# Three stages around a bounded attention layer: one block for the middle stage, weights loaded in the front, another order of steps in the attention periods

## The reference, cut to what matters

```python
h = _L0_tok_ref(x, L0_tok_W)
h = jnp.concatenate([h, _L0_txt_ref(...)], axis=1)
h = h + _L0_attn_ref(_layernorm(h), ...)
h = h + _L0_ffn_ref(_layernorm(h), ...)
```

## Time and profile before

| | |
|---|---|
| time of three runs | 2068.76, 2068.5, 2061.65 us, median 2068.5 |
| the profiled execution | 2066.16 us, span from first to last instruction 2064.1 us |
| busy share of the span | PE 70%, DVE 44%, ACT 35%, POOL 27% |
| mean granted TensorE clock | 0.788 of full |
| instructions | 33321 |

### The profile page before, as it was taken

One profiled execution on the slowest core, in us unless ns is written; L12 is line 12 of the kernel. 1 busy time (PEld: TensorE's weight loads), 2 busy tenths in 40 slices (PEclk: granted clock), 3 DMA queues, 4 the chain that ended last, 5 costly groups with the idle time before them and its releaser, 6 DMA issues.

```text
span 2064.1 us, 33321 instructions
## 1 busy us (share of the span) xinstructions
PE 1443.6 (70%) x11676; PEld 703.7 (34%) x11676; DVE 904.6 (44%) x1638; ACT 721.5 (35%) x837; POOL 552.5 (27%) x738
## 2 busy tenths in 40 slices
PE   6774203994100736998879888888898888889963
PEld 6442103994100512333333333333333333333321
DVE  1125534004753452636436545544544544643343
ACT  0100000112100003575365365365455446447640
POOL 3777202000211001223133133232322322232331
PEclk9886656996555557899799799789889889879985
DMA  6792062872031045071051052062052052044000
GB/s 106 146 192 62 9 165 95 300 264 50 0 70 9 6 80 68 17 125 23 36 87 41 22 90 43 9 110 44 10 109 44 10 99 54 10 83 63 1 13 6
DMA packets 147574, 142.94 MB, mean 69 GB/s; under 512 B 85261, under 2 KB 112693, under 8 KB 147395
## 3 DMA queue, kind: packets, MB, share of 16 engines
q1 hardware_dynamic: 133090, 136.03, 30.4%
q0 software_dynamic: 4352, 2.43, 0.7%
q10 hardware_dynamic: 9984, 2.51, 0.6%
HBM read 110.73 MB, written 25.44 MB: 66 GB/s over the span
## 4 chain that ended last, share of the span: by engine, by line
PE 39%; DVE 17%; issue 6%; SPq 2%; ACT 2%; POOL 2%; DMA 1%; DVEq 0%; POOLq 0%; ACTq 0%
PE b_pso L1656 13%; PE b_pss L1632 10%; PE b_psm L1678 4%; PE b_psm L1702 3%; PE b_psm L1690 3%; ACT b_pb L1736 2%; PE b_pss L1630 2%; DVE b_rq L1901 1%; PE b_psm L1600 1%; POOL b_pb L1776 1%; PE b_psm L1685 1%; PE b_psm L1682 1%; PE b_psm L1707 1%; DVE b_h L1900 1%; DVE b_tmp L1959 1%
## 5 line engine op out<-in xcount | busy, mean ns | idle before, releaser
L1736 ACT ACTIVATE b_pb<-b_pss 128x1024 f32<-128x1024 f32 (+2 forms) x736 | 663.5, 937 | 719.3 <-PE b_pss L1632 563.2
L1776 POOL TENSOR_SCALAR_AFFINE_SELECT b_pb<-b_pb 128x256 f32<-128x256 f32 (+1 forms) x544 | 240.4, 461 | 880.1 <-ACT b_pb L1736 873.8
L1656 PE MATMUL b_pso<-b_pb,b_vop 128*32 128x77 f32 (+4 forms) x5376 | 416.8, 420 | 71.1 <-POOL b_pb L1776 54.9
L1632 PE MATMUL b_pss<-b_qop,b_kop 97*128 97x512 bf16 (+3 forms) x1536 | 371.6, 365 | 41.1 <-issue 18.5
L1632 PEld LDWEIGHTS b_pss<-b_qop,b_kop 97*128 97x128 bf16 x1536 | 125.7, 106 | 283.5 <-ACT b_pb L1736 122.1
L1656 PEld LDWEIGHTS b_pso<-b_pb,b_vop 128*32 128x32 f32 x5376 | 118.6, 117 | 273.6 <-issue 200.5
L580 PE MATMUL psc<-tz,ub 128*32 128x128 f32 x2304 | 128.4, 278 | 75.5 <-DVE ub L613 75.5
L580 PEld LDWEIGHTS psc<-tz,ub 128*32 128x32 f32 x2304 | 127.5, 110 | 76.4 <-issue 75.7
L1982 DVE TENSOR_TENSOR b_ofm<-b_pso,b_mk 128x512 f32<-128x512 f32 (+1 forms) x96 | 51.8, 540 | 223.3 <-PE b_pso L1656 220.0
L1870 DVE COPY b_ot<-b_psm 128x336 f32<-128x336 f32 (+1 forms) x96 | 40.2, 419 | 181.1 <-PE b_psm L1678 180.9
L1757 POOL TENSOR_TENSOR b_stat<-b_stat,b_mh 128x18 f32<-128x18 f32 x32 | 107.3, 3369 | 38.8 <-DVE b_stat L2039 27.3
(11 more groups left out here) (318 smaller groups left out, 1548.7 us busy)
## 6 DMA issues: line engine op xcount, KB each, us to landing
tz<-taps SPq DMA_DIRECT2D x64, 576.0 KB, 4.7
b_qop<-qk_parts_b SPq DMA_DIRECT2D x192, 144.0 KB
stream<-in_x SPq DMA_DIRECT2D x16, 1024.0 KB, 12.7
qk_parts_b<-b_qs SPq DMA_DIRECT2D x16, 864.0 KB, 5.0
b_kop<-qk_parts_b SPq DMA_DIRECT2D x192, 36.0 KB
b_mk<-b_mskf SPq DMA_DIRECT2D x128, 36.0 KB, 3.8
qk_parts_b<-b_ks SPq DMA_DIRECT2D x8, 432.0 KB, 3.9
h<-h ACTq DMA_DIRECT2D x9, 256.0 KB, 4.1
```

The source lines that it names most:

```text
L1632: mm = pe.matmul(pss[:, u % 2, b, col:col + w], lhs, qop[:, n, e, q0:q0 + w], start=True, stop=True, skip_group_check=True)
L1656: mm = pe.matmul(pso[VW * ee:VW * (ee + 1), (3 * n + x) % 2, q0 - QT * x:q0 - QT * x + w], vop[0:r, j, n, :], pb[0:r, slot_, b, cc:cc + w] ...
L1736: nc.scalar.activation(pb[:, s % PB, 0:nb, 0:w], pss[:, s % 2, 0:nb, 0:w], ACT.Exp, scale=float(HD) ** 0.5).then_inc(exped, 1)
L1776: ins = pool.affine_select(out=v_, in_=v_, compare_op=ALU.is_ge, fill=0.0, base=0, pattern=pat, channel_multiplier=-1)
```

## The change

- **Shared tiles.** The weights of the middle and last stage are tiles that live through all stages (class `Shared`). SP loads all of them in the front (82 loads), behind the tables and ahead of the store of `taps`. DVE clears three of them at the front's start.
- **Middle stage.** One block. `wall`, `backm`, the mixer and gate constants and the turned `W_fc` are made before the convolution. ACT issues the loads of `hl`; its norm to `ul` runs nine groups a turn inside the convolution's loop, with POOL's root. The bias is a matmul of a row of ones with `brow` (384 columns) ahead of three `fc` matmuls; ACT takes the gelu from PSUM. What follows is cut into four quarters of two batches: `variance`, POOL's `root`, `scale`, and the last sum on POOL (`finish`) for the first three and on DVE for the last. `lnb` is added to `hl` beforehand. Two batches are stored per quarter.
- **Last stage.** The preamble keeps four fills and the loads. Five other fills go to POOL in period -1 (`late_ok`). The norm of `h4` and the 24 residual jobs (`RNORM`, `RES`) are steps 1 to 36 of period 0. `squares` has its own tile.
- **Step lists.** `EPI` stands in steps 24 to 42 (before 37 to 58), `PRO` in 38 to 76 (before 16 to 54), `XNORM` from 29 (before 6), `BOUND` at 78 (before 56); the query features are six steps apart per third instead of seven.
- **SP's order.** Head 0's twelve copies wait only for the spilled parts. The wait for the bound, the store of `mt` and the wait for its landing come after them.

```diff
+class Shared:
...
+        self.ident = sb("w_ident", [P, P])
+        self.wfc = sb("w_fc", [D, 2, D])
...
+                sp.wait_ge(w_zero, 3)
+                sp.dma_start(w.wha[:, 0:D], t["L0_ffn_hl_w"].rearrange("n d h -> (n d) h")).then_inc(weights, 16)
...
+                        sp.dma_start(w.gwt[32 * e:32 * e + HD, n, :], t["L0_ffn_gate_w"][n, :, HD * e:HD * e + HD].rearrange("k d -> d k"), allow_slow_non_contiguous=True).then_inc(weights, 16)
                 sp.wait_ge(kr_ok, 1)
                 sp.dma_start(krev_d, kr[:]).then_inc(kr_stored, 16)
                 sp.wait_ge(kr_stored, 16)
+                sp.wait_ge(weights, 16 * 82)
...
+                pe.transpose(psw[:, 0:D], w.wfc[:], w.ident[0:D, 0:D]).then_inc(wt, 1)
+                pe.wait_ge(psw_out, 2)
+                pe.matmul(psw[0:D + 1, 0:512], w.wha[:], w.wbd[:], start=True, stop=True).then_inc(wt, 1)
...
+                for q in range(NQ):
+                    for i in range(NT):
+                        if q:
+                            pe.wait_ge(zg, NT * (q - 1) + i + 1)
+                        pe.matmul(psf[:, i, 0:3 * P], w.ones[:], w.brow[:].rearrange("p r d -> p (r d)"), start=True, stop=False, skip_group_check=True)
+                        for a in range(3):
+                            r0 = 32 * i + B * a + 2 * q
+                            mm = pe.matmul(psf[:, i, a * P:(a + 1) * P], y1[:, r0:r0 + 2, :], wb[:], start=False, stop=True, skip_group_check=True)
...
+                act.wait_ge(s_h, 16 * B)
+                for b in range(B):
+                    act.dma_start(grp(hl, b), view(h1d, b)).then_inc(s_hl, 16)
...
+                def root(q):
+                    c = slice(GQ * q, GQ * q + GQ)
+                    pool.wait_ge(fv, q + 1)
+                    pool.tensor_tensor(stat[:, 3, c], stat[:, 2, c], mh[:, c], ALU.pow).then_inc(fr, 1)
+                def finish(q):
+                    pool.wait_ge(scaled, q + 1)
+                    pool.tensor_tensor(cut(z, q), cut(sq, q), cut(hl, q), ALU.add).then_inc(h_ok, 1)
+                root(0)
+                root(1)
+                finish(0)
+                root(2)
+                finish(1)
+                root(3)
+                finish(2)
...
+                            ln.step(red(stl[:, 0], at(hl), AX.X, ALU.add))
+                            ln.step(ts(stl[:, 1], stl[:, 0], -1.0 / D, None, ALU.mult))
+                            ln.step(tt(at(ul), at(hl), bcast(stl[:, 1], D), ALU.add))
+                            ln.step(tt(at(sq), at(ul), at(ul), ALU.mult))
+                            v.sem_inc(side, 1)
+                            ln.step(red(stl[:, 0], at(sq), AX.X, ALU.add))
+                            ts(stl[:, 2], stl[:, 0], 1.0 / D, EPS, ALU.mult, ALU.add).then_inc(lv, 1)
+                        else:
+                            v.wait_ge(lr, it + 1)
+                            v.sem_inc(side, 1)
...
+                def variance(q):
+                    st = stat[:, :, GQ * q:GQ * q + GQ]
+                    v.wait_ge(zg, NT * q + NT)
+                    ch.step(tt(cut(z, q), cut(z, q), cut(ul, q), ALU.add))
+                    ch.step(red(st[:, 0], cut(z, q), AX.X, ALU.add))
+                    ch.step(ts(st[:, 1], st[:, 0], -1.0 / D, None, ALU.mult))
+                    ch.step(tt(cut(z, q), cut(z, q), bcast(st[:, 1], D), ALU.add))
+                    ch.step(tt(cut(sq, q), cut(z, q), cut(z, q), ALU.mult))
+                    ch.step(red(st[:, 0], cut(sq, q), AX.X, ALU.add))
+                    ts(st[:, 2], st[:, 0], 1.0 / D, EPS, ALU.mult, ALU.add).then_inc(fv, 1)
+                def scale(q):
+                    v.wait_ge(fr, q + 1)
+                    ch.step(tt(cut(sq, q), cut(z, q), bcast(stat[:, 3, GQ * q:GQ * q + GQ], D), ALU.mult))
+                    tt(cut(sq, q), cut(sq, q), bmid(w.lng[:], GQ), ALU.mult).then_inc(scaled, 1)
+                variance(0)
+                variance(1)
+                scale(0)
+                variance(2)
+                scale(1)
+                variance(3)
+                scale(2)
+                scale(3)
+                v.wait_ge(scaled, NQ)
+                tt(cut(z, 3), cut(sq, 3), cut(hl, 3), ALU.add).then_inc(last_ok, 1)
...
-        PRO = [(16 + i, "turn", c) for i, c in enumerate(chunks)] + [(19, "tok", (0, 8)), (20, "tok", (8, 9))]
-        PRO += [(21 + i, "seen", i) for i in range(3)]
-        PRO += [(24 + 2 * x, "feat", (2, x)) for x in range(3)] + [(31 + x, "knorm", x) for x in range(3)]
-        for x in range(3):
-            PRO += [(35 + 7 * x, "feat", (0, x)), (37 + 7 * x, "feat", (1, x)), (40 + 7 * x, "qnorm", x)]
-        EPI = [(s_, "fturn", c) for s_, c in zip((37, 38, 40), chunks)] + [(s_, "fc1", i) for i, s_ in enumerate((43, 44, 46))]
-        EPI += [(s_, "fc2", i) for i, s_ in enumerate((49, 50, 52))] + [(s_, "back", c) for s_, c in zip((55, 58), ((0, 5), (5, 9)))]
+        PRO = [(s_, "turn", c) for s_, c in zip((38, 40, 41), chunks)] + [(43, "tok", (0, 8)), (45, "tok", (8, 9))]
+        PRO += [(46 + i, "seen", i) for i in range(3)]
+        PRO += [(s_, "feat", (2, x)) for x, s_ in enumerate((50, 52, 55))] + [(57 + x, "knorm", x) for x in range(3)]
+        for x, at_ in enumerate(((60, 62, 64), (66, 68, 70), (72, 74, 76))):
+            PRO += [(at_[0], "feat", (0, x)), (at_[1], "feat", (1, x)), (at_[2], "qnorm", x)]
+        EPI = [(s_, "fturn", c) for s_, c in zip((24, 25, 27), chunks)] + [(s_, "fc1", i) for i, s_ in enumerate((29, 30, 32))]
+        EPI += [(s_, "fc2", i) for i, s_ in enumerate((35, 36, 37))] + [(s_, "back", c) for s_, c in zip((39, 42), ((0, 5), (5, 9)))]
+        RES = [(13 + 6 * n + i, kind, (n, c)) for n in range(4) for i, (kind, c) in enumerate([("rturn", c) for c in chunks] + [("rmat", c) for c in chunks])]
-        squares = h4[:].rearrange("p a d -> p (a d)").bitcast(BF16).rearrange("p (s f) -> p s f", f=FB)
+        RNORM = (1, (6, 8), 11)
-        PUT = (40, 60, 83, 5)
-        CHECK, BOUND = 23, 56
-        FXNORM, XNORM, LASTNORM = (13, (28, 30), 34), (6, (11,), 14), (60, (64, 66), 70)
-        GATEEXP, FINISH = 74, 77
+        PUT = (47, 60, 83, 5)
+        CHECK, BOUND = 46, 78
+        FXNORM, XNORM, LASTNORM = (11, (18, 20), 23), (29, (31,), 35), (43, (51, 53), 57)
+        GATEEXP, FINISH = 60, 84
...
-                for s_, c in ((exped, 2), (summed, PB), (free, 2), (acc_free, 2), (stored, 16), (spilled, 16), (result, 1)):
+                for s_, c in ((xn_ok, 1), (exped, 2), (summed, PB), (free, 2), (acc_free, 2), (stored, 16), (spilled, 16), (result, 1)):
...
-                        sp.wait_ge(bound_ok, c + 1)
-                        sp.sem_inc(sp_passed, 1)
-                        sp.dma_start(mt_, mt[:]).then_inc(spilled, 16)
-                        sp.wait_ge(spilled, c * 64 + 80)
+                        sp.wait_ge(spilled, c * 64 + 64)
...
+                            if n == 0:
+                                sp.wait_ge(bound_ok, c + 1)
+                                sp.sem_inc(sp_passed, 1)
+                                sp.dma_start(mt_, mt[:]).then_inc(spilled, 16)
+                                sp.wait_ge(spilled, c * 64 + 80)
+                                sp.sem_inc(sp_passed, 1)
...
-                                sp.wait_ge(const_ok, 1)
+                                sp.wait_ge(late_ok, 5)
...
-                pe.wait_ge(weights, 16 * (NW + 4 * NH))
-                gate(0)
-                job(0, lambda: pe.matmul(bank()[0:D + 1, 0:512], wha[:], wbd[:], start=True, stop=True))
...
-                for n in range(4):
-                    for c in chunks:
-                        turn_rows(h4[:, NA * n:NA * (n + 1)], c, 0)
-                    for c in chunks:
-                        gate(0, c[0] == 0)
-                        for a in range(*c):
-                            mm = pe.matmul(bank()[:, (a - c[0]) * HD:(a - c[0] + 1) * HD], xt[:, a * P:(a + 1) * P], wall[:, 448 + HD * n:464 + HD * n], start=True, stop=True)
...
+                    if kind == "rturn":
+                        n, c = c
+                        pe.wait_ge(rn_ok, 1)
+                        turn_rows(h4[:, NA * n:NA * (n + 1)], c, base)
...
+                    elif kind == "rmat":
+                        n, c = c
+                        gate(base, c[0] == 0)
+                        for a in range(*c):
+                            mm = pe.matmul(bank()[:, (a - c[0]) * HD:(a - c[0] + 1) * HD], xt[:, a * P:(a + 1) * P], wall[:, 448 + HD * n:464 + HD * n], start=True, stop=True)
...
+                    if att and not prev:
+                        pe.wait_ge(late_ok, 5)
...
+                    if not att and not prev:
+                        pool.wait_ge(rstd, 1)
+                        pool.memset(kop[KT:KB_], -1.0).then_inc(late_ok, 1)
+                        pool.wait_ge(late_ok, 1)
...
+                        pool.memset(ot[:], 1.0).then_inc(late_ok, 1)
...
```

(17 more changed lines are left out.)

587 lines of the change are left out of this document (278 added, 309 removed).

## The result

The changed kernel takes 1881.3 us (median of 4 runs, 1873.1 to 1885.8), the kernel before in the same session 2065.1. The ratio is 0.911, with an interval of 0.907 to 0.916. The forecast was 1821, its range 1785 to 1898: the time lies inside the range, 60 us above the forecast. The profiled execution of the changed kernel took 1883.3 us, its span is 1881.5.

What follows compares the result with a forecast made beforehand. PE was taken to bound the attention periods, with two serial stretches before them. From 2064.1: minus 68 (middle stage), 84 (preamble), plus 2 (prologue), minus 11 (period 0), 84 (six periods) gives 1819, forecast 1821 us; range 1785 to 1898.

Steps and rivals of the forecast that it cites:

- the likeliest case: Whole kernel: the forecast of 1821 us itself, chance 50%, said to span 1795 to 1850 us alone.
- the clock stays low: Rival for the periods: low clock due to kind of jobs, not alternation; 75 us not gained, 1896 us; chance 26%.
- The preamble: Last stage, up to the first reduction of `hb`: 93.1 us shrink to 9, gain 84 us.
- The stall of period 0: Period 0: PE's stall of 17.95 us behind the late load of `hb` goes, minus 18 us.
- three signs that the prediction named for its own failure: Period's mean clock stays at 0.85, PE's first score of a period waits for `b_qop`, or POOL's sums exceed 5 us.
- Four quarters are 38 us; add ...: 41.2: Middle stage's DVE chain: four quarters 38 us, plus 0.8 last root, 1.3 last sum, 1.3 second-quarter wait.
- With 2.1 it hides beside DVE: Middle stage: a quarter sum on POOL takes 2.1 us by the nearest row and hides beside DVE.
- the 9 us given back by the clock: Period 0: 21 busy low-clock us at full rate give 9 us back, within the net minus 11.
- the 30.5 busy microseconds at 1.2 GHz would shrink by 15; I take 11: Periods 1 to 6: PE's low-clock stretch with alternating `feat` and `fc` jobs speeds up, gaining 11 us a period.
- which I put at 1.6: Periods 1 to 6: DVE crowded at steps 57 to 66, MIX among its work, costing 1.6 us a period.
- The deadline: Head 0 for the next period: 2 to 3 us late, hidden by PE's 3.76 us pause at the loop's start.
- Head 0 comes late: Rival at period starts: DVE's crowding delays the last feature 5 to 8 us, PE stands; 1869 us; chance 14%.

Runs made afterwards that it cites:

- the steps alone: Kernel before with only the new step lists, norms and their order of waiting for roots; ratio 0.987, period 0 134.7 us, six periods 934.7 us.
- the session of 2182.1 us: Session of e1_old_order and three other runs, in which the kernel before took 2182.1 us; in the next session it took 2061.9.
- the unrolled kernel with the sums on DVE: Changed kernel with bound stored early, first pair's MIX at step 88, six-period loop written out, and middle-stage quarter sums on DVE, not POOL; ratio 0.867.
- the early bound: Changed kernel with the bound stored ahead of head 0's copies and waited for only behind them; ratio 0.915, six periods 924.6 us.
- e1_old_order: Changed kernel with SP's old order, bound stored and waited for ahead of head 0's copies; ratio 0.913, six periods 926.6 us.

## Why the prediction was right, and where it was not

**The number.** 1881.3 us lies in the range of 1785 to 1898, but outside the 1795 to 1850 that the likeliest case alone was said to span, and 15 us below the 1896 of the rival "the clock stays low", which had 26%. The verdict of faster was right for its reasons, as the stretches outside the loop gave what was forecast; the loop gave less than half.

**Right, to a few us.** The preamble (84 forecast, 85.4). The prologue (2, and 0.8). The stall of period 0 (18; in the steps alone it is gone), and the residual jobs (13.7, and 14.1). The end of `fc` behind `feat`: no `b_rq` wait under an `fc` is left. The first normalisation hides under the convolution. The loads in the front cost next to nothing: the front is 3.4 us longer here, and between 0 and 3.4 in the other runs with the same front outside the session of 2182.1 us. Of the three signs that the prediction named for its own failure two came, the mean clock that stays near 0.85 and the first score that waits for `b_qop`; POOL's sums stayed under 5 us. The number lies in the range because the rivals of the loop were priced into it.

**The middle stage,** 68 forecast, 59.2 measured. Its start was right: the first variance comes 206.4 us into the stage, where the forecast has 207.4. The step that failed is "Four quarters are 38 us; add ...: 41.2" (its own terms give 41.4); the chain takes 50.3 (498.3 to 548.6). The quarters by themselves take 39.9, as an operation lasts 1.36 us and not 1.24. The waits for the second quarter's gelu and for the last root take 2.1 and 1.7 us where the forecast has 1.3 and 0.8; POOL's pow lasts 4.27 there and not 3.37. And "With 2.1 it hides beside DVE" fails: a sum takes 2.60 us, and the operation beside it is held up, twice by 1.43 us and once by 2.4, 5.3 in all. The Trainium skill, "GPSIMD Engine Reference", sections "Engine selection" and "Key points", had both halves: two-input work at half VectorE's pace, and SBUF interfaces shared with VectorE's operations that have two SBUF inputs or run in a 2-port mode. The trace agrees with the pace (2.60 against 1.36 us) and with a hold-up, which is larger than the 2 us that were estimated from the page. The operation held up by 2.4 us has two inputs; the two held up by 1.43 have one, and no run shows in which mode they ran. The forecast's sum went by the nearest row instead.

**Period 0,** 11 forecast, 6 measured. The term that failed is the 9 us given back by the clock: with the steps alone PE's busy time falls by 4.2 us. Two waits that the forecast did not have for this period, 3.1 us for `b_ofm` and 3.4 for the row, take more than that, and small gains elsewhere (some 3 us) bring the sum to the 1 us beyond the stall.

**The six periods,** 84 forecast, 32 measured. Three terms.

First, "the 30.5 busy microseconds at 1.2 GHz would shrink by 15; I take 11". The mean clock stayed, 0.84 after 0.85. The reading was too large to begin with: the five slices hold 30 us of the lower level, and PE was idle in 4.5 of their 35 us. The low stretch was laid to `feat` and `fc` alternating; they no longer do, and there is one all the same at steps 43 to 50, now with `turn`, `back` and `tok` at its start. Moving `turn` and `tok` away from there ended it (0.96 over the period, six periods from 843.8 in the unrolled kernel with the sums on DVE to 803.8). So the rival that put the low clock on the kind of jobs and not on alternation was the better one, with other jobs than it had in view. With them went the norm on DVE, POOL's root and the load of `hb`; that it is the jobs on PE and none of these is argued, not shown. What makes `tok` harmless at step 20 and not at step 53 was not settled: at 53 a wait of 1.07 us stood in front of it. That the jobs of the kernel before let the clock fall by the same road was not tried.

Second, the crowding of DVE, "which I put at 1.6". It was seen and listed, MIX by name, and costs 9.3: 3.3 us of wait and some 5 of low clock behind it. What was missed is that a wait of PE has a second price.

Third, head 0. The deadline was worked out as 2 to 3 us late and hidden by the pause at the loop's start. The row comes up to 1.5 us behind the end of PE's branch, and PE waits 1.4 us more in the mean than with the early bound (6.4 against 5.0). The rival "Head 0 comes late" would have been confirmed by reading the waits alone; the early bound shows that it was worth 1 us a period or less. The pause itself was taken as given, as one in which PE waits for nothing shown. It is PE's branch back, 4.6 us in the mean before and 6.4 in the changed kernel, and the edge was the larger item: 5.7 us each. Why the branch takes longer with the new steps was not tried; it does in the steps alone too (5.4 to 7.1 us).

On the clock's rule in the Trainium skill, "TensorE: Matmul & The Clock Gate", section "What's actually happening" (low is the default, sustained activity releases it): the runs agree as far as the falls behind waits go, at 1347, at 1383 and at each loop edge. They agree less in the stretch with `tok`, where the table of the changed kernel has PE busy for 7.00 of 7 us at 0.50. There moving `turn` and `tok` away helped, and no wait was removed.

## What to carry to other kernels

Price a wait of the bounding engine twice: its length, and the stretch at the lower clock behind it (3.3 us of wait cost 9.3 here). Where such a wait is at a loop's edge, look at the engine's own branch record, or write the loop out once, before shortening what the table of waits names as the releaser. And when a job moves to another step, follow the load that feeds it and every queue that its root stands in: the gain of the clock was first eaten by a load at the end of SP's queue.

## What the hardware showed that was not expected

- PE's branch back took 4.5 to 4.8 us in the kernel before and 5.3 to 7.3 in the changed one, in a loop of some 150 us a turn with all engines in it; leaving the loop took 0.08, and the branches of ACT, POOL and SP under 0.06. With the low clock behind it an edge cost 5.7 us. The Trainium skill, "Advanced Engine Details and Errata", section "Control Flow Timing", has 51 ns for a branch and 108 ns for a compare and branch. That is the order of the short ones here; for PE's branch back the measurement decides. What PE's sequencer does in that time no run shows.
- DVE is held up beside a POOL sum: a product of 1.35 us took 3.76 and a scaling of 0.18 took 1.61. The reverse is seen and was not tried alone: POOL's pow of 18 values took 4.27 us beside DVE's work, with and without the sums, where the first, at 505.7, took 3.22 with DVE idle for 2 us of it.
- The bound's store landed 5.5 us after its issue (the median) when it stood behind twelve copies, 2.1 ahead of them in `e1_old_order`, and 1.6 in the kernel before.
